# A decoder layer in one kernel: attention probabilities turned by transposing transfers, and the Toeplitz rows loaded in three parts

## What is computed

```
# mixer: 16 heads, softmax over positions, weights depend on i - j only
z = softmax(einsum('bse,he->bsh', x, W_A) * SCALING, axis=1)
roll = zp[:, :, (i - j) % S] * tril
out = einsum('bhij,bjhd->bihd', roll, v);  x = x + out @ W_O.T + b_O
# cross-attention, one head, causal
score = einsum('bqd,bkd->bqk', Q, K) / sqrt(dk)      # masked where k > q
x = x + einsum('bqk,bkd->bqd', softmax(score), V)
# network: 2 shared experts, 16 routed ones of which each row takes 2
x = x + shared(x) + routed(x)
```

## Time and profile before

| what | value |
|---|---|
| median of three runs | 587.88 us (586.95, 587.88, 588.98) |
| profiled execution: its span, which is also the one time kept of it | 587.6 us |
| PE busy | 556.6 us, 95% |
| DVE busy | 443.4 us, 75% |
| ACT busy | 235.1 us, 40% |
| POOL busy | 181.9 us, 31% |
| all traffic of SP's queue | 94.09 MB, 57.1% of the 16 engines' span |

### The profile page before, as it was taken

How to read it: one execution, slowest core, us unless ns; L and a number is a source line. 1 busy time by engine, 2 the same in 40 slices (tenths; PEclk the granted TensorE clock), 3 DMA queues, 4 the chain that set the end, 5 groups by cost and what they waited for, 6 DMA issues and landing times. The chain is left out here.

```text
span 587.6 us, 13723 instructions
## 1 busy us (share of the span) xinstructions
PE 556.6 (95%) x5164; PEld 378.9 (64%) x5164; DVE 443.4 (75%) x1132; ACT 235.1 (40%) x463; POOL 181.9 (31%) x223
## 2 busy tenths in 40 slices
PE   6888889999999999999999999999999999999997
PEld 5566567566685666766686667666766666566455
DVE  5858688768975788868886898769876777677754
ACT  3555544443344243343344333342443323432332
POOL 4215150222532145123523333224421341223123
PEclk8979999999999999999999999999999999999999
DMA  8995595892439913595439831892269226400251
GB/s 251 291 362 191 182 387 171 183 348 99 109 79 230 343 34 89 122 268 178 108 76 241 258 107 54 176 345 79 67 135 301 77 78 123 87 2 1 72 111 37
DMA packets 90737, 94.75 MB, mean 161 GB/s; under 512 B 28224, under 2 KB 76224, under 8 KB 90432
## 3 DMA queue, kind: packets, MB, share of 16 engines
q1 hardware_dynamic: 90688, 94.09, 57.1%
HBM read 75.66 MB, written 12.12 MB: 149 GB/s over the span
## 5 line engine op out<-in xcount | busy, mean ns | idle before, releaser
L652 POOL TENSOR_TENSOR mid<-gated,mid 128x512 f16<-128x512 f32 x72 | 86.4, 1200 | 242.8 <-ACT mid L813 242.7
L813 ACT ACTIVATE mid<-gated 128x512 f16<-128x512 f32 x72 | 45.1, 626 | 108.5 <-DVEq L1123 108.5
L145 PE MATMUL wide<-w_d,mid 128*128 128x256 f16 x288 | 78.6, 273 | 0.0
L147 PE MATMUL wide<-w_d,mid 128*128 128x256 f16 x288 | 78.5, 273 | 0.0
L146 PE MATMUL wide<-w_d,mid 128*128 128x256 f16 x288 | 78.5, 273 | 0.0
L1104 DVE SCALAR_TENSOR_TENSOR gated<-gated,score 128x512 f32<-128x512 f32 x72 | 49.1, 682 | 36.4 <-ACT gated L808 35.2
L145 PE MATMUL score<-h3T,w_gu 128*128 128x512 f16 x160 | 60.7, 380 | 0.9 <-DVEq L125 0.8
L146 PE MATMUL rows<-h3T,w_gu 128*128 128x512 f16 x160 | 60.7, 380 | 0.0
L145 PE MATMUL rows<-h3T,w_gu 128*128 128x512 f16 x160 | 60.7, 380 | 0.0
L147 PE MATMUL score<-h3T,w_gu 128*128 128x512 f16 x160 | 60.7, 379 | 0.0
L146 PE MATMUL score<-h3T,w_gu 128*128 128x512 f16 x160 | 60.7, 379 | 0.0
(11 more groups left out here) (224 smaller groups left out, 1372.7 us busy)
## 6 DMA issues: line engine op xcount, KB each, us to landing
toep<-z_scratch SPq DMA_DIRECT2D x14, 2048.0 KB, 17.7
stage<-comb_scratch SPq DMA_DIRECT2D x32, 512.0 KB, 8.5
toep<-z_scratch SPq DMA_DIRECT2D x4, 1024.0 KB, 11.6
x_bo<-in_x SPq DMA_DIRECT2D x8, 512.0 KB, 11.6
x_in<-in_xr SPq DMA_DIRECT2D x7, 512.0 KB, 11.6
qT<-q_scratch SPq DMA_DIRECT2D x7, 512.0 KB, 3.9
vx<-v_scratch SPq DMA_DIRECT2D x7, 512.0 KB, 5.3
out<-x_out SPq DMA_DIRECT2D x7, 512.0 KB, 3.0
```

What stands on the lines that cost most here:

```text
L145: pe.matmul(out, stationary[0], moving[0], start=start, stop=False, **kw)
L147: return pe.matmul(out, stationary[1], moving[0], start=False, stop=stop, **kw)
L652: pool.tensor_tensor(mid_slot(j, 1, late), gate_slot(j, late), mid_slot(j, 0, late), ALU.subtract).then_inc(mid_split.sem, 1)
L813: act.activation(mid_slot(j, 0, late), gate_slot(j, late), ACT.Copy).then_inc(mid_hi.sem, 1)
```

## The change

The probabilities are no longer turned by PE. ACT and DVE split `prob` as it stands (rows of queries) into fp16 halves, in space borrowed from `h2` (`prob_parts`), and SP turns them with four transposing transfers (`move_prob`, c = 0 to 3, of 2 (c+1) blocks of 128x128) into `probT`, which now holds all four blocks side by side. The fp32 transposes and their place in the PSUM rota go. `attend(c)` waits for the landing of transfer c. ACT and DVE do the splits of blocks 0 and 1 together at j = 3, block 2 at j = 4 and block 3 at j = 5 (it waits for transfer 1, whose source it overwrites). Half a = 0 of the Toeplitz rows is loaded at its old place, ahead of the four transfers; half a = 1 is cut in two loads of 8 heads (1 MB each), one behind transfer 1 and one behind transfer 2.

```diff
+            def move_prob(b, c):
+                hold(sp, prob_split, prob_split.at(b, c + 1))
+                sp.dma_start(probT_parts(c).rearrange("p (n s) -> p n s", s=P), prob_parts(c), transpose=True).then_inc(prob_moved[c].sem, 16)
...
                     if m:
                         sp.wait_ge(mix_ready.sem, mix_ready.at(it - 1, 2))
+                        load_toeplitz(it, 0, slice(0, H), toep_loaded.sem)
...
                 if f and m and not d:
                     store_context(2)
-                    store_context(3)
-                    load_context(6)
-                    store_context(4)
-                    store_context(5)
                 if c is not None:
                     store_context(c)
                     if c + 1 < B:
                         load_context(c + 1)
+                if m:
+                    if f and not d:
+                        sp.wait_ge(ctx_stored[1], 32)
+                    move_prob(it - 1, 0)
+                    move_prob(it - 1, 1)
+                if f and m:
+                    load_toeplitz(it, 1, slice(0, H // 2), toep_loaded.sem)
+                if f and m and not d:
+                    store_context(3)
+                    load_context(6)
+                if m:
+                    move_prob(it - 1, 2)
+                if f and m:
+                    load_toeplitz(it, 1, slice(H // 2, H), toep_loaded.sem)
+                if m:
+                    move_prob(it - 1, 3)
+                if f and m and not d:
+                    store_context(4)
+                    store_context(5)
                 if f and m:
                     fetch_context(it, it)
...
-            def part_prob(it, b, c):
-                act.wait_ge(turned.ready.sem, turned.is_ready(it, f"pt{c}"))
+            def part_prob(b, c):
+                act.wait_ge(prob_ready.sem, prob_ready.at(b, c + 1))
+                if c == C - 1:
+                    act.wait_ge(prob_moved[1].sem, prob_moved[1].at(b, 16))
+                act.activation(half_of(prob_parts(c), 0), prob[:, c % 2, 0:P * (c + 1)], ACT.Copy,
+                               scale=X_P).then_inc(prob_hi.sem, 1)
...
-            def turn_probs(it, b, c):
-                turned.fill(pe, it, f"pt{c}")
-                pe.wait_ge(prob_ready.sem, prob_ready.at(b, c + 1))
-                for t in range(c + 1):
-                    last = pe.transpose(turned.bank(f"pt{c}")[:, P * t:P * t + P], prob[:, c % 2, P * t:P * t + P],
-                                        ident[:])
-                last.then_inc(turned.ready.sem, 1)
+            def attend(it, b, c):
+                turned.fill(pe, it, f"p{c}")
+                pe.wait_ge(prob_moved[c].sem, prob_moved[c].at(b, 16))
```

More of the change, by code:

```diff
@@ L53 @@
 X_MID = 16.0
[L57 to L58 removed]
+TURNED = ["mix.0", "mix.1", "combT", "h2.0", "h2.1", "p0", "p1", "p2", "p3", "h3.0", "h3.1", "h1.0", "h1.1", "none"]
 SCORE = ["z", "g0", "g1", "g2", "s0", "s1", "g3", "s2", "g4", "s3", "g5", "g6", "g7", "g8", "g9", "none"]
@@ L218, in decoder_layer @@
         prob = sb("prob", [P, 2, S])
-        probT = sb("probT", [P, 2, 2, S], F16)
+        probT = sb("probT", [P, P * C * (C + 1)], F16)
         h3 = sb("h3", [P, C, E])
@@ L380, in decoder_layer @@
         prob_scaled = sig("prob_scaled", C)
-        probT_hi = sig("probT_hi", C)
+        prob_hi = sig("prob_hi", C)
+        prob_split = sig("prob_split", C)
+        prob_moved = [sig(f"prob_moved{c}", 16) for c in range(C)]
         x_kept = sig("x_kept", 1, 1)
@@ L435, in mid_slot, with prob_parts, probT_parts, half_of @@
             return mid[:, half, j % SLOTS]
+        def prob_parts(c):
+            at = 2 * P * (7, 0, 4, 0)[c]
+            return h2[:].rearrange("p c e -> p (c e)").bitcast(F16)[:, at:at + 2 * P * (c + 1)]
+        def probT_parts(c):
+            return probT[:, P * c * (c + 1):P * (c + 1) * (c + 2)]
+        def half_of(t, a):
+            return t.rearrange("p (a s) -> p a s", a=2)[:, a]
         def context_unit(n, u, half):
@@ L569, in iteration @@
                         sp.wait_ge(mix_ready.sem, mix_ready.at(it - 1, 2))
[L571 to L577, removed]
+                        load_toeplitz(it, 0, slice(0, H), toep_loaded.sem)
+                    else:
+                        for g in range(2):
+                            for a in range(2):
+                                load_toeplitz(it, a, slice(H // 2 * g, H // 2 * g + H // 2),
+                                              toep_loaded.sem if g else first_toep_loaded)
                 if f and not m:
@@ L922, in iteration @@
                         part_mid(it - 2, j - 1)
+                    if m and j == AHEAD:
+                        part_prob(it - 1, 0)
+                        part_prob(it - 1, 1)
                     if d:
@@ L1080, in score_sum, with part_prob @@
                 dve.reciprocal(s_rsum[:, c:c + 1], s_scaled[:, c:c + 1]).then_inc(score.taken.sem, 1)
-            def part_prob(it, b, c):
-                turned.take(dve, it, f"pt{c}")
-                dve.wait_ge(probT_hi.sem, probT_hi.at(b, c + 1))
-                n = P * (c + 1)
-                dve.scalar_tensor_tensor(probT[:, 1, c % 2, 0:n], turned.bank(f"pt{c}")[:, 0:n], X_P,
-                                         probT[:, 0, c % 2, 0:n], ALU.mult, ALU.subtract).then_inc(turned.taken.sem, 1)
+            def part_prob(b, c):
+                dve.wait_ge(prob_hi.sem, prob_hi.at(b, c + 1))
+                hi, lo = (half_of(prob_parts(c), a) for a in range(2))
+                dve.scalar_tensor_tensor(lo, prob[:, c % 2, 0:P * (c + 1)], X_P, hi, ALU.mult,
+                                         ALU.subtract).then_inc(prob_split.sem, 1)
             def attended(it, c):
@@ L1331, in iteration @@
                         normalise(it - 1, it, 2, x_res, h3, 1)
+                    if m and not at:
+                        part_prob(it - 1, 0)
+                        part_prob(it - 1, 1)
                     if d:
@@ L1340, in iteration @@
                         normalise(it - 1, it, 2, x_res, h3)
-                    if m and at < C:
-                        part_prob(it, it - 1, at)
+                    if m and 1 <= at < C - 1:
+                        part_prob(it - 1, at + 1)
                     if first and j in CONTEXT_BEFORE:
@@ L1693, in iteration @@
                         if d and 0 <= at - 1 < C:
-                            attend(it, at - 1)
+                            attend(it, it - 1, at - 1)
                         if j - 1 < C:
```

24 lines of the change are left out of this document (11 added, 13 removed).

## The result

The changed kernel takes **607.22 us** (median of 4 runs, 605.93 to 609.85) against 588.07 us (4 runs, 586.95 to 588.98) for the kernel before, run beside it: a ratio of **1.032**, 95% interval 1.029 to 1.036. The forecast was 603.0 us, 589 to 611. The profiled execution of the changed kernel took 606.22 us, with a span of 604.4 us, 16.8 more than before. The forecast's sum, +15.2, is to be held against these 16.8; the rest of the way from the forecast 603.0 to the median 607.22 is that the profiled execution was 1.0 us faster than the median of its runs, and that its time lies 1.8 us above its span, of which the forecast had put in 0.3.

A forecast was written before the change was run, and what follows sets the result against it. PE was taken as the bound, busy 556.6 of 587.6 us. Terms: -7.7 transposes, +10.0 and +0.3 waits, +9.2 iteration 1, +3.4 clock; +15.2 gives 602.8, forecast 603 us, range 589 to 611.

The forecast's parts named there:

- Iterations 4 to 7, the new wait.: Before `attend` of block 0, PE waits for a transfer queued behind Toeplitz rows: 3.7, 2.8, 2.2, 1.3 us, sum 10.0.
- The queue works in order.: DMA transfers, transposing ones included, land in issue order, so block 0's lands 0.3 us after the first Toeplitz half.
- Iteration 1.: PE stands 7.8 us for the first transfer and 4.1 us for the third; net +9.2 us, saved transposes included.
- The clock.: TensorE's granted clock falls after two of the four waits in iterations 4 to 7, 1.7 us each: +3.4 us.
- What PE saves.: Ten transposes an iteration leave PE, 0.11 us each: 1.1 us an iteration, 8.8 over eight, 7.7 outside iteration 1.
- iterations 2, 3 and 8: Wait for block 0's transfer: 0.3 us in iteration 2, iteration 3 even, no Toeplitz rows in 8; +0.3 us together.
- The splits, later blocks, the late rows.: First two splits (0.7 us) hide in DVE's idle 1.62 us; later transfers from iteration 2 and late Toeplitz rows cost nothing.
- (b): Rival: transfers slip past the queued Toeplitz rows, landing 3.0 us after issue; no `attend` waits; 578.8 us; chance 0.08.
- (c): Rival: queue order holds but waits are half as long and the clock stays up; 591.9 us, 588 to 596; chance 0.10.
- (d): Rival: the clock falls at every wait and stays down longer; 613 us; chance 0.05.
- (e): Rival: transposing transfers are slow, 0.38 us a block even behind others; 610 us; chance 0.03.

The follow-up runs named there:

- `ahead_later`: Changed kernel, but iterations 2 to 7 issue transfers of blocks 0 and 1 before the first Toeplitz half, block 2 right behind it, block 3 later: 597.42 us.
- `other_queue`: Changed kernel, with the first Toeplitz half issued by ACT from its own queue, all else on SP's: 606.51 us, ratio 1.033.
- `before_pool`: Kernel before, with DVE's subtraction `h1p<-x_in,h1p` moved to POOL, nothing else changed: 584.63 us, ratio 0.995.
- `filled`: Changed kernel, with ten useless 512-column matmuls ahead of the wait for block 0's transfer in iterations 4 to 7: 602.71 us, ratio 1.024.
- `unturned`: Changed kernel without the four transfers: halves written straight into `probT`, so attend uses untransposed probabilities: 585.17 us, ratio 0.994.
- `unturned_pool`: Changed kernel with neither transposes nor transfers (probabilities left unturned), and DVE's subtraction `h1p<-x_in,h1p` moved to POOL: 580.04 us, ratio 0.985.
- `toep_split`: Kernel before, with its second Toeplitz half loaded in two pieces behind the context stores, the second once block 2 is taken from PSUM: 595.77 us.
- `best3`: Changed kernel with transfers issued early, DVE's `h1p` subtraction on POOL, and the queue reordered in iterations 1 to 3: 580.60 us, ratio 0.988.
- `ahead_first`: Changed kernel, but iteration 1 alone issues transfers of blocks 0 and 1 before the first Toeplitz half, block 2 right behind it, block 3 later: 600.80 us.

## Why the prediction was right, and where it was not

**Iterations 4 to 7, the new wait.** Right. Forecast 3.7, 2.8, 2.2 and 1.3 us, 10.0 together; measured 3.1, 2.4, 2.5 and 2.6, 10.5 together. The landing 0.3 us after the Toeplitz half was right to 0.1 us (in iteration 4). The shape was not: "a wait does not shrink the next one" holds, but the decline over the iterations, taken from the earlier trace rows, didn't appear; iteration 7's term was half its size. `ahead_later`, which takes just these waits away, puts the periods at 62.8.

**"The queue works in order."** Right as an observation, incomplete as a reason. `ahead_later` shows that a transfer issued before the rows isn't late (2.3 us to its landing), and `other_queue` that one issued while they are in flight in another queue is late too (6.7 us). The load on the shared engines suffices; with the order in the queue on top it was 7.3 us.

**Iteration 1.** Near in its total, +10.0 against +9.2, in part by luck. PE started at 78.12, on a landing forecast for 78.0. PE was there 2.1 us earlier than forecast (78.12 - 10.01 = 68.1) and stood 10.0 instead of 7.8 us; the second stand was 2.4 instead of 4.1, so that the errors made each other good. The early arrival has little to do with the change. The arrival in the earlier trace rows, 70.57, was late by what the first 45 us of that one execution had lost: a wait of 2.0 us for the first Toeplitz rows and 6.8 us of half clock behind it. In `before_pool`, which does the same work up to there without a fall, `attend` of block 0 starts at 68.81. Held against its period of 61.58, iteration 1 of the changed kernel is 11.1 us longer.

**The clock.** Mis-sized by one fall: three of them, not two, after the waits of iterations 5, 6 and 7. The price of each, 1.7 us, was right for these: `filled` gives back 4.5 us in the time, 4.7 in the periods. The place from which it was taken, the fall near the start in the earlier trace rows, would have given less: by the first marks of the fourteen traces that fall delays PE by only 0.5 to 1.0 us. The price of a fall is not one number in this kernel.

**What PE saves.** This is the term that was mis-sized, at 7.7 us (8.8 with iteration 1). "Whatever PE no longer does comes off the time" is wrong in this kernel: `unturned` measures all of it at 3.5 us, with 0.05 us in a steady period; 0.65 us of it lies in iteration 7 and 1.6 us behind the last mark. DVE's chain ended last there already, as the 0.59 us wait for `h3T` in the kernel before says, so what PE no longer did turned into waits: 0.79 us for `mid`, and 0.92 for 0.59. `unturned_pool` shows that DVE is the cause: with 1.19 us taken from DVE the wait for `mid` is gone and the period is 1.08 us shorter. Where PE has stood for a transfer, DVE has caught up meanwhile, and then the saving is real and the wait for `h3T` goes too. Iteration 5 of the changed kernel has only the one wait of 2.36 us, so its +2.11 is 2.36 + 1.7 for the clock - 1.1 - 0.59 = 2.4, near enough.

Set against the sum of +15.2: iterations 4 to 7 came out at +8.7, where -4.4 + 10.0 + 3.4 = +9.0 had been forecast (one fall more, and 0.5 us more of waits, about made good by older waits that went: 1.8 us are the three for `h3T` in iterations 4 to 6, and 0.7 us are not traced); iteration 1 at +10.0 for +9.2; iterations 2, 3 and 8 at 0.6 - 0.2 - 1.6 = -1.2 for 0.3 - 3.3 = -3.0, since no transfer is waited for long in them (0.4 us in iteration 2) and DVE's chain, as `unturned` suggests, took the savings; and 0.7 us less ahead of the first mark, which is the fall near the start that this execution didn't have. Together +1.6, which makes 16.8.

**The splits, later blocks, the late rows.** Hidden, as forecast, though the first two splits had been mis-sized: 1.49 us together instead of 0.7, nearly all of the 1.62 us of cover, and DVE is busy for 452.0 instead of 443.4 us. No `attend` of blocks 1 to 3 waits from iteration 2 on, and `toep_split` shows no cost of late rows from iteration 3 on. In iteration 1 the change's own rows land in good time, as said there.

**The rivals.** (b) falls with the landings: 7.3 us after the issue instead of 3.0. (c) falls with waits of 10.5 us in iterations 4 to 7 and three falls of the clock, (d) with no fall in iteration 4 and falls of 3.4 us in the others. (e) needed block 0's transfer to land 0.8 us behind the rows, and it landed 0.3 us behind them. If the 1309 ns that the Trainium skill gives for a 128x128 turn by DMA (VectorE: DVE Perf Modes, "The three transpose paths") were a rate, the eight blocks of block 3 would take 10.5 us, an estimate, and be late in every iteration. This case's traces disagree with it as a rate: in iteration 4 the eight blocks landed 3.1 us after their issue, and PE never waits for them from iteration 2 on. The same page of the Trainium skill ("Rules for kernel authors") advises TensorE for such a turn where the result may go to PSUM. The pair `before_pool` and `best3` gives the measure of that here: 584.63 us with the turns on TensorE, 580.60 with the transfers well placed. So here they are worth moving, by 4 us of 588, and only so placed; `best3` differs from `before_pool` in the order of some stores and loads too.

## What to carry to other kernels

A small transfer that an engine waits for must be issued before the bulk loads that share its engines, not merely in another queue; price it by the landing of what is in flight, and check every consumer of what is pushed back. Price removed work not by an engine's busy share but by how far behind it the next engine's chain ends: look for the second-longest wait, and take from both at once. And a wait of TensorE costs more than its length where the clock falls after it.

## What the runs showed of the hardware that wasn't expected

- The longest wait of the steady iterations, 3.08 us in iteration 4, had no fall of the clock behind it; 2.36, 2.47 and 2.58 us in iterations 5 to 7 had one each, of 3.4 us at 0.50. In `other_queue` it was the other way round: a fall at 2.85 us in iteration 4, none at 2.3, 2.0 and 2.0. What decides was not settled. In the four runs of `ahead_first` the span largely goes with the mean granted clock: 593.4 us at 0.997, 598.5 at 0.986, 599.5 at 0.982, 601.2 at 0.983.
- Two DMA queues on the same engines share them: in iteration 4 a transposing transfer of two 128x128 fp16 blocks took 6.7 us beside a 2 MB load in another queue, 7.3 us behind one in its own, and 2.3 us with neither.
- DVE's split of 128x128 probabilities took 1.15 us in the seven iterations in which it ran beside an operation of POOL (1.16 us), and 0.27 us in the one in which it didn't.
- Ten useless matmuls in the place of a wait made the kernel 4.5 us faster.
